# Eight cores, a recurrent mixing layer: output statistics taken inside the last projection stage, six accumulation banks and one casting engine

## The reference

```python
xn = _layernorm(x)                                   # x: (2, 4096, 2048)
prev = concatenate([xn[:, 1:2], xn[:, :-1]], 1); xx = prev - xn
r = (xn + xx*tm_r) @ Wr.T
k = (xn + xx*tm_k) @ Wk.T
v = (xn + xx*tm_v) @ Wv.T
g = sigmoid((xn + xx*tm_g) @ Wg.T)
wkv = _wkv_scan(k, v, exp(-exp(time_decay)), time_first)   # over time
o = (sigmoid(r) * wkv * g) @ Wo.T
s = (o - mean(o)) * rsqrt(var(o) + 1e-5) * ln_g + ln_b     # over the 2048 channels
g2 = silu(xn @ ternary(W_ffn).T + bias)
y = x + s * g2
```

## Time and profile before

| | |
|---|---|
| median of 3 runs | 1457.35 us (1448.6 to 1464.92) |
| profiled execution, its own time | 1448.6 us |
| span of its slowest core (core 4), which the profile shows | 1447.0 us |
| r/g/o block | 752 to 1299.6 us |
| statistics block, its summing part | 1299.6 to 1333.0 us |
| rest of the statistics and the output block | 1333.0 to 1447.0 us |

### The profile page before, as it was taken

The page is one execution under the profiler, slowest core; times in us unless marked ns, Lnnn a source line. Parts: engine busy times, 40 slices in busy tenths (PEclk is TensorE's granted clock), DMA queues, the critical chain, the costliest instruction groups (busy, mean ns, idle before and its releaser), DMA issues. The chain is left out here.

```text
span 1447.0 us, 11739 instructions; the slowest of 8 cores (1435.6 to 1447.0 us)
## 1 busy us (share of the span) xinstructions
PE 820.1 (57%) x3762; PEld 362.0 (25%) x3834; DVE 538.3 (37%) x531; ACT 474.3 (33%) x628; POOL 104.2 (7%) x196
## 2 busy tenths in 40 slices
PE   3542220038949379999950875270596879885200
PEld 1110000014525135544420332130242334331000
DVE  0158998300000001767007055595310111101597
ACT  4532222112222122122212357467253322238221
POOL 0002222100000000011110000000000000000001
PEclk9555555569979689999985897795698999988555
DMA  4447889684251741655127432533624444400487
GB/s 128 135 134 251 258 260 255 183 240 151 88 195 42 244 159 60 187 166 177 39 79 228 126 120 85 149 123 104 182 85 128 123 130 130 126 2 1 116 241 223
DMA packets 79069, 211.64 MB, mean 146 GB/s; under 512 B 11424, under 2 KB 11424, under 8 KB 79008
## 3 DMA queue, kind: packets, MB, share of 16 engines
q1 hardware_dynamic: 54432, 139.57, 33.8%
q0 software_dynamic: 15360, 53.49, 10.3%
q10 hardware_dynamic: 9216, 17.83, 3.8%
HBM read 166.81 MB, written 39.85 MB: 143 GB/s over the span
## 5 line engine op out<-in xcount | busy, mean ns | idle before, releaser
L984 PE MATMUL rgo_ps<-mov_rg,rgo_wbf 128*128 128x512 bf16 x1003 | 233.3, 394 | 189.5 <-DMA mov_rg<-sxg 61.5
L405 PE MATMUL g1ps<-mov_kv,g1wbf 128*128 128x512 bf16 (+1 forms) x1505 | 260.3, 335 | 105.4 <-DMA mov_kv<-sxk 45.9
L829 ACT ACTIVATE rgo_wbf<-rgo_mw 128x512 bf16<-128x512 f32 x160 | 100.3, 632 | 288.1 <-DMA rgo_mw<-wo 97.2
L405 PEld LDWEIGHTS g1ps<-mov_kv,g1wbf 128*128 128x128 bf16 x1536 | 133.2, 101 | 232.4 <-issue 117.7
L984 PEld LDWEIGHTS rgo_ps<-mov_rg,rgo_wbf 128*128 128x128 bf16 x1024 | 102.5, 101 | 320.3 <-issue 208.6
L984 PE MATMUL rgo_ps<-wkv_sb,rgo_wbf 128*128 128x512 bf16 x502 | 117.2, 395 | 15.6 <-ACT sr_sb L960 7.7
L405 PE MATMUL g1ps<-xn_sb,g1wbf 128*128 128x512 bf16 x502 | 110.2, 380 | 0.5
L269 DVE CAST g1wbf<-g1mwstg 128x1024 bf16<-128x1024 f32 x24 | 16.7, 694 | 241.8 <-PE g1ps L405 93.6
L333 ACT ACTIVATE g1row<-g1ps 128x512 f16<-128x512 f32 (+1 forms) x96 | 44.6, 492 | 149.0 <-PE g1ps L405 136.7
L573 PE MATMUL ps_sc<-fs_a,ones 128*1 128x512 f16 x64 | 32.3, 609 | 88.0 <-ACT fs_a L618 88.0
L984 PEld LDWEIGHTS rgo_ps<-wkv_sb,rgo_wbf 128*128 128x128 bf16 x512 | 51.6, 101 | 81.2 <-issue 25.3
(11 more groups left out here) (113 smaller groups left out, 816.3 us busy)
## 6 DMA issues: line engine op xcount, KB each, us to landing
g1mwstg<-wf SPq DMA_DIRECT2D x64, 512.0 KB, 4.4
g1mwstg<-wk SPq DMA_DIRECT2D x32, 512.0 KB, 6.8
g1mwstg<-wv SPq DMA_DIRECT2D x32, 512.0 KB, 4.6
rgo_mw<-wr SPq DMA_DIRECT2D x64, 256.0 KB, 3.3
rgo_mw<-wg SPq DMA_DIRECT2D x64, 256.0 KB, 3.3
rgo_mw<-wo SPq DMA_DIRECT2D x64, 256.0 KB, 3.2
xstg<-x SPq DMA_DIRECT2D x16, 576.5 KB, 3.8
xst<-x SPq DMA_DIRECT2D x16, 512.0 KB, 5.6
```

Of the source, the lines that this page charges most:

```text
L405: mm = e.matmul(bank[:, :t1 - t0], wbf[hh % 2][:, ic, oc * 128:(oc + 1) * 128], s["mov"][:, ic, t0:t1], start=(ic == 0), stop=(ic == CH - 1))
L829: e.activation(wbf[ss % 2][:, ic, :], mwstg[jj % 2][:, :], AF.Copy).then_inc(sem["scs"], 1)
L984: mm = e.matmul(bank[:, :t1 - t0], wbf[ss % 2][:, ic, oc * 128:(oc + 1) * 128], phs[p]["mov"][:, ic, t0:t1], start=(ic == 0), stop=(ic == ...
```

## The change

1. The r/g/o block has 6 banks `ps` in place of 8. The two others, `qsa` and `qsb`, hold the four rows of sums of the statistics, at partitions 0 and 32 of each.
2. All Wo casts are ACT's. DVE has no casts in this block any more.
3. The statistics' copy and square are emitted in ACT's queue of the r/g/o block, after the second evacuation of each output block of p = 2. From the third output block on, ACT first waits until TensorE has summed the block two before (`sm2`), since `oh16` and `oq16` have two buffers.
4. TensorE sums output block oc - 2 behind the groups of output block oc (`stats_mm`), and the last two after all groups.
5. The arithmetic on mean and deviation is appended to the queues of DVE and ACT in the r/g/o block. The statistics block is gone.

```diff
         ps = [ec(nc.psum_tensor("rgo_ps%d" % i, [128, 512], F32))
-              for i in range(8)]
+              for i in range(6)]
+        qsa = ec(nc.psum_tensor("qsa", [128, 512], F32))
+        qsb = ec(nc.psum_tensor("qsb", [128, 512], F32))
+        qs1 = [qsa[32 * j:32 * j + 1, :] for j in range(len(TC_OWN))]
+        qs2 = [qsb[32 * j:32 * j + 1, :] for j in range(len(TC_OWN))]
...
             for ic in range(CH):
-                if ss >= 2 * NSLAB and ic % 2 == 0:
-                    cv += 1
-                    castrec.append(("V", "scv", cv))
-                else:
-                    cs_ += 1
-                    castrec.append(("S", "scs", cs_))
+                cs_ += 1
+                castrec.append(("S", "scs", cs_))
...
                     inc(e.activation(sr_sb[:, ocg, t0:t1], bank[:, :t1 - t0],
                                      AF.Copy), "sev")
+                    if tj == ntc - 1:
+                        if ocg >= 2:
+                            e.wait_ge(sem["sm2"], b["sm2"] + ocg - 1)
+                        e.drain()
+                        e.activation(oh16[ocg % 2][:, :], sr_sb[:, ocg, :],
+                                     AF.Copy)
+                        inc(e.activation(oq16[ocg % 2][:, :],
+                                         sr_sb[:, ocg, :], AF.Square), "ss")
...
+        def stats_mm(e, ci):
+            e.wait_ge(sem["ss"], b["ss"] + ci + 1)
+            for j, (t0, t1) in enumerate(TC_OWN):
+                e.matmul(qs1[j][:, :t1 - t0], ones16[:, :],
+                         oh16[ci % 2][:, t0:t1],
+                         start=(ci == 0), stop=(ci == CH - 1))
+                mm = e.matmul(qs2[j][:, :t1 - t0], ones16[:, :],
+                              oq16[ci % 2][:, t0:t1],
+                              start=(ci == 0), stop=(ci == CH - 1))
+            inc(mm, "sm2")
...
                             inc(mm, "smm")
+                            if (p == 2 and tj == ntc - 1
+                                    and 0 <= sl * OSL + oc - 2):
+                                stats_mm(e, sl * OSL + oc - 2)
+            stats_mm(e, OSL * NSLAB - 2)
+            stats_mm(e, OSL * NSLAB - 1)
```

More of the change, by code:

```diff
@@ L58, in build_nc @@
     sem = {n: e0(nc.semaphore(n)) for n in
-           ("sl", "sw0", "sw1", "scv", "scs", "smm", "sev", "st0", "st1",
-            "sv", "ss", "sden", "srd", "sg0", "sg1")}
+           ("sl", "sw0", "sw1", "scv", "scs", "smm", "sm2", "sev", "st0",
+            "st1", "sv", "ss", "sden", "srd", "sg0", "sg1")}
     cnt = {n: 0 for n in sem}
@@ L721, in build_nc @@
     es_o = contextlib.ExitStack()
+    oh16 = [es_o.enter_context(nc.sbuf_tensor("oh16_%d" % i, [128, T_OWN],
+                                              F16)) for i in range(2)]
+    oq16 = [es_o.enter_context(nc.sbuf_tensor("oq16_%d" % i, [128, T_OWN],
+                                              F16)) for i in range(2)]
+    stv = es_o.enter_context(nc.sbuf_tensor("stv", [1, T_OWN], F32))
+    stm = es_o.enter_context(nc.sbuf_tensor("stm", [1, T_OWN], F32))
+    stq = es_o.enter_context(nc.sbuf_tensor("stq", [1, T_OWN], F32))
     sr_sb = es_o.enter_context(
@@ L789, in build_nc @@
                 v_events.append(("sr", cj))
[L790 to L795, removed]
+        for k in range(NGp):
+            v_events.append(("gmul", k))
         svord = {}
@@ L799, in build_nc @@
         for kind, l in v_events:
-            if kind not in ("chain", "vcast"):
+            if kind != "chain":
                 i += 1
@@ L907, in _ @@
                                         sr_sb[:, l, :], OP.mult), "sv")
-                elif kind == "gmul":
+                else:
                     _p, sl_g, oc_g, tj_g = g_info(NR + l)
@@ L917, in _ @@
                                         OP.mult), "sv")
-                else:
-                    emit_cast(e, l)
+            e.wait_ge(sem["sm2"], b["sm2"] + CH)
+            for j, (t0, t1) in enumerate(TC_OWN):
+                e.tensor_scalar(stm[:, t0:t1], qs1[j][:, :t1 - t0],
+                                1.0 / C, None, OP.mult)
+                e.tensor_scalar(stv[:, t0:t1], qs2[j][:, :t1 - t0],
+                                1.0 / C, None, OP.mult)
+            e.drain()
+            e.tensor_tensor(stq[:, :], stm[:, :], stm[:, :], OP.mult)
+            e.drain()
+            e.tensor_tensor(stv[:, :], stv[:, :], stq[:, :], OP.subtract)
+            e.drain()
+            inc(e.tensor_scalar(stv[:, :], stv[:, :], LN_EPS, None,
+                                OP.add), "sv")
+            e.wait_ge(sem["ss"], b["ss"] + CH + 1)
+            e.drain()
+            inc(e.tensor_tensor(stm[:, :], stm[:, :], stv[:, :], OP.mult),
+                "sv")
         @blk.scalar
@@ L996, in build_nc @@
         ec = es.enter_context
[L997 to L1003, removed]
         rb2 = ec(nc.sbuf_tensor("rb2", [128, T_OWN], F32))
@@ L1007, in build_nc @@
                for i in range(2)]
[L1009 to L1056, removed]
-                e.drain()
-                inc(e.tensor_scalar(stv[:, :], stv[:, :], LN_EPS, None,
-                                    OP.add), "sv")
-                e.wait_ge(sem["ss"], b["ss"] + CH + 1)
-                e.drain()
-                inc(e.tensor_tensor(stm[:, :], stm[:, :], stv[:, :], OP.mult),
-                    "sv")
```

6 lines of the change are left out of this document (added).

## The result

The changed kernel takes 1493.2 us (median of 12 runs, 1480.2 to 1513.6); the kernel before took 1459.1 us in its 12 runs. The ratio is 1.0249 with a 95% interval of 1.020 to 1.030. The change makes the kernel slower by 2.5% in the ratio; the medians lie 34.1 us apart. The profiled execution took 1499.4 us, and its slowest core is core 5 with a span of 1497.9 us.

The account below looks back on a forecast made before the run. From slab 6 on ACT's queue was the bound: casts, chained to landings, plus evacuation. Terms 1.4 + 6.4 + 8.1 + 6.6 + 16.3 + 14.0 - 16.7 = +36.1 us on 1457.35 made 1493 us, range 1472 to 1510.

Parts of the forecast that it names:

- p = 0: Slabs before slab 5's phase, where ACT's 23.5 us of reciprocals cover the wait for banks: no cost.
- casts plus evacuation: ACT's loop per slab: casts of 30.7 us, a chain of landings, then evacuation, which is paid in full.
- The banks: With six banks two groups wait for ACT's evacuation phase, which grows from 3.7 to 10.3 us; period 41.0 us.
- T5 to T6: From the last weight cast of slab 5 to that of slab 6: 1.4 us longer.
- T7 to T8: From the last weight cast of slab 7 to that of slab 8: 32.9 us becomes 41.0, 8.1 longer.
- Casts by ACT: Wo cast phases with ACT alone: 0 to 1.6 us more per slab, taken near the upper bound at 30.7 us.
- The statistics in p = 2: Copies and squares in the Wo slabs' evacuation phases: TensorE restarts at 3.4 us, phase 16.4 us, period 47.1 us.
- T9 to T10: From the last weight cast of slab 9 to that of slab 10: 32.1 us becomes 48.4, 16.3 longer.
- the table load of 1.3 us: One change from Sigmoid's tables to Square's, in the first evacuation phase with statistics: 1.3 us.
- Behind T11: After slab 11's last weight cast: its matmuls start at 14.3 us, last sum at 48.6 instead of 65.3, gaining 16.7.
- the landings did not get quicker: Rival in the cast phases: quicker landings take most of the loss back, to 1475 or 1465 us; chance 0.12.
- the rival with the low clock: TensorE runs groups 6 and 7 wholly at 1.2 GHz, 4.8 us more per phase, 6 times: 1522 us; chance 0.07.

## Why the prediction was right

**What bounds the kernel.** That from S6 on the loop is ACT's queue, a chain of landings and then evacuation, held in every run with two staging buffers. Lengthening the evacuation or shortening the casts moved the time at once, while giving work back to DVE moved it by some 5 us. Spreading the casts between the evacuations gained much in the changed kernel, but in the kernel before only in p = 0. So "casts plus evacuation" is the right sum for the order in which ACT does them, but not the price of the evacuation: a landing runs beside it. With six banks that makes no difference to the forecast, since both buffers are full long before the longer evacuation ends.

**The banks.** Evacuation phases of 10.3 us were forecast and 10.3 to 10.6 us measured (mean over the cores) behind T6, T7 and T8; the kernel with six banks alone confirmed the term by itself. T5 to T6 came out at the forecast +1.4. That p = 0 pays nothing also held: T1 to T5 is the same to 0.2 us, with the reciprocals as cover. The term for T7 to T8 was 1.7 us too large: 1.2 of it because I took 32.9 us for the period before from one core and the mean over the cores is 34.1, the rest because the period came out at 40.5 and not 41.0.

The Trainium skill (Perfetto Trace Analysis, Matmul Optimizations) says to use all 8 PSUM banks. The runs agree for this loop (8 to 6 costs 42.7 us). They also bound it: with four staging buffers the kernel that gives two banks to the sums was the faster one. The changed kernel too fills all eight banks, six with groups and two with sums, so the rule by itself does not forecast its loss. The bank count alone was not changed with four staging buffers.

**Casts by ACT.** Within 0 to 1.6 us a slab, as bounded: 2 to 4 us in sum in two pairs of kernels, near the noise. I had put the term down to the slower cast; the distances put it down to the later start of the Wo casts.

**The statistics in p = 2.** The order of events was as written: TensorE released by the square at 3.2 us (3.4 forecast), last pair at 15.7 us (16.4). T9 to T10 came out at +12.4 for +16.3. Of these 3.9 us, 1.5 are the period before (32.1 us on core 4, 33.6 in the mean); the period after was 46.0 us for 48.4. Its evacuation phase took 15.8 us where 17.7 were forecast, and two sizes in it were off. The first is the table load of 1.3 us, which is not there: the Square of line 986 runs behind Copy and Sigmoid without a load, and the load stands before the Ln instead, behind the sums:

```profile
1389.17 0.68 DVE L932 TENSOR_SCALAR stv<-stv 1x1024 f32<-1x1024 f32 x1
1389.92 1.28 ACT L991 ACT_TABLE_LOAD   x1 [6.84 <-DVE stv L932]
1391.22 1.06 ACT L991 ACTIVATE stv<-stv 1x1024 f32<-1x1024 f32 x1
```

So two steps of the prediction failed by this load, in opposite directions: the 1.3 us in the first phase are not there, and what follows the last sum does not have "the same instructions" (112.8 us before, 114.2 after). The Ln starts at 1391.22, 1.30 us after the load began, as in the earlier trace rows; the further drain of 1.38 us that the Trainium skill gives (ScalarE: Activation LUTs, What ACT_TABLE_LOAD costs) is again not seen. The second is the four small matmuls. I took 1.7 us at the low clock and 0.86 us at full clock; they take 0.95 at the low clock until the next group starts, and 0.43 to 0.53 at full clock, see below.

**Behind T11.** 48.6 us were forecast and 47.1 measured: S11 started 13.4 us behind T11 and not 14.3 (mean of the six cores with complete records), and the way from the last evacuation to the last sum took 2.8 us and not 3.5. Before, it was 65.3 us on core 4 and 63.6 in the mean. That the gain of 16.7 us came out at 16.5 is luck, since both numbers were some 1.6 us too large.

**The sum.** 36.1 us forecast, 32.0 in the stretch from T5 to the last sum of the two profiled executions, and 34.1 us between the medians. Of the 4 us missing in the stretch, 2.4 are in T9 to T10 and 1.5 behind T11. That the median fell on the 1493 us forecast is partly luck: the added time was 2 us less, and the median before, over 12 runs, 2 us more than the 1457.35 I started from. No rival took a part: the mean cast phases from S6 on were 29.6 to 31.4 us, so the landings did not get quicker with longer pauses, and TensorE's restart cost 2.2 and 2.7 us in the two rows shown (29.80 and 30.39 us for 128 matmuls of 0.216). The 2.7 is over the 2.1 that I had set as a limit, but far from the 4.8 more of the rival with the low clock.

## What to carry to other kernels

Before buffers are taken from a loop to hide work elsewhere, look at which engine hands them back and what else stands in its queue: here ACT freed the banks only behind 30 us of casts, so the loop needed as many banks as TensorE fills in that time, and two fewer cost 43 us while hiding the statistics gave back 15. The same change gained 13 to 23 us, from the first cast to the last sum, once the cast phase was short or interleaved. A chain of "cast, then load, then wait 3.3 us" is a matter of how many loads are under way, so a few KB more of staging can be worth more than a reordering (2.5% for the one tried on the kernel before). It was worth 7.4% here, for 4 KB a partition.

## What the hardware showed that was not expected

The four small matmuls of a sum, which write one PSUM row each, overlap in the changed kernel. Behind the last group they look like this (the two matmuls of one line write partitions 0 and 32 of one bank). The program issues them in the order `qsa`, `qsb`, `qsa`, `qsb`, and the records start in the order `qsa`, `qsa`, `qsb`, `qsb`:

```profile
1380.23 0.38 PE L998 MATMUL qsa<-oh,ones 128*1 128x512 f16 x2
...
1380.45 0.38 PE L1001 MATMUL qsb<-oq,ones 128*1 128x512 f16 x2
1380.66 0.38 PE L998 MATMUL qsa<-oh,ones 128*1 128x512 f16 x2
1380.88 0.39 PE L1001 MATMUL qsb<-oq,ones 128*1 128x512 f16 x2
```

A sum of four takes 0.43 us (1380.23 to 1380.66) where the four of the earlier trace rows, all at partition 0, took 0.86. In the seven-bank kernel, with rows at partitions 0, 32, 64 and 96, all four start within 0.01 us:

```profile
1240.86 0.38 PE L997 MATMUL qsa<-oh,ones 128*1 128x512 f16 x1
1240.86 0.38 PE L1000 MATMUL qsa<-oq,ones 128*1 128x512 f16 x1
1240.87 0.38 PE L997 MATMUL qsa<-oh,ones 128*1 128x512 f16 x1
1240.87 0.38 PE L1000 MATMUL qsa<-oq,ones 128*1 128x512 f16 x1
```

and the next group starts 0.32 us after them. Such matmuls run side by side when their outputs lie in different quarters of the partitions. The Trainium skill states this (TensorE: Matmul & The Clock Gate, Part 3: Packing small matmuls — row/col tiling), and these rows agree.

Also not expected: with two 256 KB loads in flight the DMA traffic in a cast phase was some 0.65 of what four reached (120 to 135 against 195 to 204 GB/s on core 4), at a landing that grew only from 3.3 to 4.2 us.
